# Top-8 replacement, exponentials and masks of the first expert layer by token quarter, with masks on GpSimd in both layers

## What is computed

```python
logits = jnp.einsum('bsd,ed->bse', x, gate_w) + gate_b
probs = jax.nn.softmax(logits, axis=1)                 # over the 4096 tokens
vals, idx = jax.lax.top_k(probs.transpose(0, 2, 1), K)  # K = 8
...
pooled = jnp.einsum('bked,bke->bed', gathered, topv)   # weighted sum of the 8 tokens
h = jax.nn.gelu(...pooled, weight1...)
out = ...h, weight2...
weighted = jnp.einsum('beo,bke->bkeo', out, topv)      # scattered back to the 8 tokens
```

## Time and profile before

| | before |
|---|---|
| device time, median of 3 runs | 574.76 us (574.59 to 575.63) |
| the profiled execution's own time | 575.6 us |
| its span in the profile | 573.8 us |
| TensorE busy | 533.4 us (93%) |
| VectorE busy | 333.3 us (58%) |
| ScalarE busy | 296.9 us (52%) |
| GpSimd busy | 63.6 us (11%) |

### The profile page before, as it was taken

One profiled execution on the slowest core, in us unless ns is written; L12 is line 12 of the kernel. 1 busy time (PEld: TensorE's weight loads), 2 busy tenths in 40 slices (PEclk: granted clock), 3 DMA queues, 4 the chain that ended last, 5 costly groups with the idle time before them and its releaser, 6 DMA issues.

```text
span 573.8 us, 26756 instructions
## 1 busy us (share of the span) xinstructions
PE 533.4 (93%) x11432; PEld 494.5 (86%) x11432; DVE 333.3 (58%) x826; ACT 296.9 (52%) x762; POOL 63.6 (11%) x62
## 2 busy tenths in 40 slices
PE   8889899899997999899999999989999999977895
PEld 8889899899996895689999999989999999976782
DVE  2767686635459926874445444434544455389826
ACT  4556575732278502465555555576666555567300
POOL 4000000020021000000000033320000044640000
PEclk9999999999999888999999999999999999999978
DMA  9941782330000000000000024330000244410007
GB/s 353 376 149 55 270 336 83 137 159 2 1 2 0 2 22 0 2 1 3 2 0 0 4 61 103 76 39 3 0 0 2 47 76 70 78 29 1 2 3 292
DMA packets 48159, 40.80 MB, mean 71 GB/s; under 512 B 42554, under 2 KB 42810, under 8 KB 46877
## 3 DMA queue, kind: packets, MB, share of 16 engines
q1 hardware_dynamic: 46606, 37.27, 20.2%
q0 software_dynamic: 1344, 2.17, 1.8%
q10 hardware_dynamic: 144, 0.39, 0.2%
HBM read 27.49 MB, written 4.19 MB: 55 GB/s over the span
## 4 chain that ended last, share of the span: by engine, by line
PE 70%; DVE 18%; ACT 3%; SPq 2%; POOL 2%; issue 2%; DMA 1%; DVEq 0%; ACTq 0%
PE PS L769 34%; PE PS L557 6%; PE PS L469 4%; PE PS L430 4%; PE PS L603 3%; PE PS L686 3%; PE PS L633 3%; PE PS L762 3%; DVE sums L1084 2%; PE PS L537 2%; DVE RCD L1096 2%; PE PS L463 2%; PE PS L496 2%; DVE sums L966 2%; SPq L332 2%
## 5 line engine op out<-in xcount | busy, mean ns | idle before, releaser
L769 PE MATMUL PS<-RE,conv_sb 128*64 128x64 f32 x6048 | 228.7, 227 | 2.5 <-DVE RE L1198 2.0
L769 PEld LDWEIGHTS PS<-RE,conv_sb 128*64 128x64 f32 x6048 | 211.0, 137 | 11.7 <-DVE RE L1198 4.4
L1198 DVE SCALAR_TENSOR_TENSOR RE<-PS,RE 128x64 f32<-128x64 f32 x504 | 113.1, 225 | 120.9 <-PE PS L769 110.3
L762 PE MATMUL PS<-ones_bf,biasT 128*64 128x64 bf16 x1008 | 100.5, 192 | 0.5 <-DVE RE L1191 0.4
L902 ACT ACTIVATE RE<-RCD 128x128 f32 (+1 forms) x126 | 38.9, 310 | 52.1 <-DVE RE L1198 52.0
L762 PEld LDWEIGHTS PS<-ones_bf,biasT 128*64 128x64 bf16 x1008 | 60.0, 112 | 1.5 <-ACT RCD L798 0.5
L469 PE MATMUL PS<-warm 128*128 128x128 bf16 x524 | 39.1, 241 | 4.0 <-DVE ones_bf L961 1.5
L469 PEld LDWEIGHTS PS<-warm 128*128 128x128 bf16 x524 | 35.3, 109 | 5.4 <-ACT RB L882 1.6
L321 POOL DMA_DIRECT2D RE<-RCD x32 | 18.6, 588 | 181.7 <-ACT RCD L905 181.7
L902 ACT ACTIVATE RE<-RE 128x128 f32 (+1 forms) x63 | 26.6, 422 | 19.5 <-DVE RE L1198 17.2
L905 ACT COPY RB<-RE 128x128 f32 (+1 forms) x126 | 35.6, 283 | 1.5 <-DVE RE L1198 1.5
(11 more groups left out here) (120 smaller groups left out, 753.0 us busy)
## 6 DMA issues: line engine op xcount, KB each, us to landing
RE<-wspec SPq DMA_DIRECT2D x8, 2048.0 KB, 9.0
RA<-x_in SPq DMA_DIRECT2D x8, 512.0 KB, 7.4
RCD<-x_in SPq DMA_DIRECT2D x1, 4096.0 KB, 13.2
out<-RA SPq DMA_DIRECT2D x8, 512.0 KB, 3.5
RCD<-RB SPq DMA_DIRECT2D x48, 64.0 KB, 2.1
RCD<-RB SPq DMA_DIRECT2D x26, 32.0 KB, 1.9
conv_sb<-conv_w SPq DMA_DIRECT2D x1, 768.0 KB, 20.0
RE<-RCD SPq DMA_DIRECT2D x8, 96.0 KB, 4.1
```

The source lines that it names most:

```text
L762: pe.matmul(conv_bank(u, h)[MO * o:MO * (o + 1)], biasT[:, s, MO * o:MO * (o + 1)], ones_bf[:, :], start=True, stop=False)
L769: m = pe.matmul(conv_bank(u, h)[MO * o:MO * (o + 1)], conv_sb[:, s, d, MO * o:MO * (o + 1)], prev, start=False, stop=(d == 2))
L1198: dve.scalar_tensor_tensor(out=state[:, state_slot(s, u), k, 1:1 + HO], in0=conv_bank(u, h), scalar=0.0, in1=rowb[:, u, k], op0=ALU.max, o ...
```

## The change

In the first expert layer (`l == 0`):

- The one replacement over 4096 tokens becomes four over 1024. A replacement by value needs a list of 8 values to look for, and a quarter's list may hold only values that are chosen in it. Three instructions on 32 elements a partition make the four lists at once: the top 8 are replaced in a copy of `cand` (`unpicked`), the rest is turned into `MASKED` and the replaced ones into 0, and this is added to `cand` (`picks`). Each has to wait for the one before.
- The exponentials are taken by quarter, in the order 0, 2, 1, 3, each with its own sum in `expsum4`; a reduction adds the four, and `rsum` is made after the mask of quarter 1.
- Between the exponentials of quarters 0 and 2, ScalarE takes the exponential of `L2` of quarter 2 in place: zero where `MASKED` stands, and equal to `E` elsewhere. GpSimd then forms this quarter's weights as the difference `E - exp(L2)`.
- VectorE's order is: replacements 2 and 0, mask 0, replacement 1, mask 1, the sum and its inverse, scaling 0, replacement 3, mask 3, scalings 1, 2, 3.
- TensorE has 76 matmuls in its `keep_warm` in place of 110. It turns `rsum` after quarter 1 and its 14 warm matmuls, and spreads it after the turning of quarter 2.

In the second layer the replacement and the exponentials stay whole. ScalarE adds the exponentials of `L2` for quarters 2 and 3, GpSimd forms those two masks, and VectorE has only masks 0 and 1 ahead of its scalings. The order on TensorE is the one from before.

The diff, without the declarations of the new tiles and semaphores and three lines that call `masks(0)`, `masks(1)` and `wait_masked`:

```diff
@@ -256,6 +260,26 @@
         CW = (E, RC[:, TOK:2 * TOK])
+        POOL_MASKS = ((2,), (2, 3))
+        DVE_MASKS = ((0, 1, 3), (0, 1))
+        REPLACED = (2, 0, 1, 3)
+        EXPS = (0, 2, 1, 3)
+
+        def wait_masked(eng, l, g):
+
+            if g in POOL_MASKS[l]:
+                eng.wait_ge(s_mskp, len(POOL_MASKS[0]) * l + POOL_MASKS[l].index(g) + 1)
+            else:
+                eng.wait_ge(s_msk, len(DVE_MASKS[0]) * l + DVE_MASKS[l].index(g) + 1)
+
+        def wait_replaced(eng, l, g):
+
+            eng.wait_ge(s_rep, 5 if l else REPLACED.index(g) + 1)
+
+        def wait_exps(eng, l, g):
+
+            eng.wait_ge(s_exp, 5 if l else EXPS.index(g) + 1)
+
         def centred(l, g):
             return RB[:, 1024 * (7 - g):1024 * (8 - g)] if l else RA[:, 1024 * g:1024 * g + 1024]
@@ -338,6 +362,13 @@
             x2 = by_run(RC[:, TOK * bh:TOK * (bh + 1)], k).rearrange("p (o i) w -> p o i w", i=Q)
             eng.tensor_tensor(X3[:, k, bh], CO[:, k, :, :, bh].rearrange("p i w o -> p o i w"), x2,
                               ALU.add).then_inc(done, 1)
+
+        def mask(eng, l, g, done):
+
+            left, exps = part(L2, l, g), part(E, l, g)
+            chosen = CW[l][:, 1024 * g:1024 * g + 1024]
+            eng.scalar_tensor_tensor(out=run_rows(chosen) if l else chosen, in0=left, scalar=MASKED / 2,
+                                     in1=exps, op0=ALU.is_le, op1=ALU.mult).then_inc(done, 1)
         block = ctx.enter_context(nc.Block())
@@ -392,6 +423,14 @@
                     xc = centred(l, g)
                     pool.tensor_tensor(square[:, 1, 0:1024], xc, xc, ALU.mult).then_inc(s_sqp, 1)
+            def masks(l):
+                for n, g in enumerate(POOL_MASKS[l]):
+                    wait_exps(pool, l, g)
+                    pool.wait_ge(s_exl, len(POOL_MASKS[0]) * l + n + 1)
+                    chosen = CW[l][:, 1024 * g:1024 * g + 1024]
+                    pool.tensor_tensor(run_rows(chosen) if l else chosen, part(E, l, g), part(L2, l, g),
+                                       ALU.subtract).then_inc(s_mskp, 1)
+
             def split_bias():
                 pool.wait_ge(s_mix, 4 * 6)
                 pool.memset(brow, 0.0).then_inc(s_bz, 1)
@@ -671,9 +712,13 @@
                     group(G_LT[l] + g, [LT[:, 8 * g + n].rearrange("p h n -> p (h n)") for n in range(8)], None)
                 pe.wait_ge(s_ld, 4 * l + 4)
-                keep_warm(0, 110)
-                pe.wait_ge(s_rs, l + 1)
-                pe.transpose(PS[0:1, 6, 0:P], rsum[:, :], ident).then_inc(s_rt, 1)
+                def turn_rsum():
+                    pe.wait_ge(s_rs, l + 1)
+                    pe.transpose(PS[0:1, 6, 0:P], rsum[:, :], ident).then_inc(s_rt, 1)
+
+                keep_warm(0, 110 if l else 76)
+                if l == 1:
+                    turn_rsum()
                 def pool_tokens(g):
                     pe.wait_ge(s_wtd, 4 * l + g + 1)
@@ -697,7 +742,9 @@
                     m.then_inc(s_wt, 1)
                     if g < 2:
                         keep_warm(7, 14)
-                    if g == 1:
+                    if l == 0 and g == 1:
+                        turn_rsum()
+                    if g == 2 - l:
                         pe.wait_ge(s_rr, l + 1)
                         pe.matmul(PS[0:C, 7, 0:P], ones[:, :], rs_row[:, :], start=True, stop=True).then_inc(s_rb, 1)
                     if g >= 1:
@@ -882,7 +929,21 @@
                     act.activation(o, i, ACT.Identity, bias=gateb_sb[:, l:l + 1]).then_inc(s_ld, 1)
                 act.wait_ge(s_nm, l + 1)
-                act.activation(E, L[l], ACT.Exp, bias=negmax[:, :], accum_out=expsum[:, :]).then_inc(s_exp, 1)
+                def exps_of_left(g):
+                    left = part(L2, l, g)
+                    wait_replaced(act, l, g)
+                    act.activation(left, left, ACT.Exp, bias=negmax[:, :]).then_inc(s_exl, 1)
+
+                if l == 0:
+                    for n, g in enumerate(EXPS):
+                        act.activation(part(E, 0, g), part(L[0], 0, g), ACT.Exp, bias=negmax[:, :],
+                                       accum_out=expsum4[:, g:g + 1]).then_inc(s_exp, 1)
+                        if n == 0:
+                            exps_of_left(2)
+                else:
+                    act.activation(E, L[l], ACT.Exp, bias=negmax[:, :], accum_out=expsum[:, :]).then_inc(s_exp, 1)
+                    for g in POOL_MASKS[1]:
+                        exps_of_left(g)
                 act.wait_ge(s_rt, l + 1)
                 act.copy(rs_row[:, :], PS[0:1, 6, 0:P]).then_inc(s_rr, 1)
                 act.wait_ge(s_rb, l + 1)
@@ -1116,16 +1177,33 @@
                 dve.max(top8[:, :], cand[:, :]).then_inc(s_mx, 1)
                 dve.wait_ge(s_mx, l + 1)
                 dve.tensor_scalar(negmax[:, :], top8[:, 0:1], -1.0, None, ALU.mult).then_inc(s_nm, 1)
-                dve.match_replace(L2, top8[:, :], L[l], MASKED).then_inc(s_rep, 1)
-                dve.wait_ge(s_exp, l + 1)
-                dve.reciprocal(rsum[:, :], expsum[:, :]).then_inc(s_rs, 1)
-                dve.wait_ge(s_rep, l + 1)
-                def mask(g):
-                    left, exps = part(L2, l, g), part(E, l, g)
-                    chosen = CW[l][:, 1024 * g:1024 * g + 1024]
-                    dve.scalar_tensor_tensor(out=run_rows(chosen) if l else chosen, in0=left, scalar=MASKED / 2,
-                                             in1=exps, op0=ALU.is_le, op1=ALU.mult).then_inc(s_msk, 1)
-
+                def total_exps():
+                    dve.wait_ge(s_exp, 4)
+                    dve.tensor_reduce(expsum[:, :], expsum4[:, :], AX_X, ALU.add).then_inc(s_sel, 1)
+                    dve.wait_ge(s_sel, 4)
+                    dve.reciprocal(rsum[:, :], expsum[:, :]).then_inc(s_rs, 1)
+
+                if l == 0:
+                    dve.match_replace(unpicked[:, :], top8[:, :], cand[:, :], MASKED).then_inc(s_sel, 1)
+                    dve.wait_ge(s_sel, 1)
+                    dve.tensor_scalar(unpicked[:, :], unpicked[:, :], MASKED / 2, MASKED, ALU.is_gt,
+                                      ALU.mult).then_inc(s_sel, 1)
+                    dve.wait_ge(s_sel, 2)
+                    dve.tensor_tensor(picks[:, :], unpicked[:, :], cand[:, :], ALU.add).then_inc(s_sel, 1)
+                    dve.wait_ge(s_sel, 3)
+                else:
+                    dve.match_replace(L2, top8[:, :], L[l], MASKED).then_inc(s_rep, 1)
+                    dve.wait_ge(s_exp, 5)
+                    dve.reciprocal(rsum[:, :], expsum[:, :]).then_inc(s_rs, 1)
+
+                def replace(g):
+                    dve.match_replace(part(L2, 0, g), picks[:, 8 * g:8 * g + 8], part(L[0], 0, g),
+                                      MASKED).then_inc(s_rep, 1)
+
+                def mask_now(g):
+                    wait_replaced(dve, l, g)
+                    wait_exps(dve, l, g)
+                    mask(dve, l, g, s_msk)
                 def weigh(g):
                     dve.wait_ge(s_wt, 4 * l + g + 1)
@@ -1135,19 +1213,24 @@
                                       .unsqueeze(4).to_broadcast([P, 8, BH, BL, NE]),
                                       ALU.mult).then_inc(s_wtd, 1)
-                mask(0)
-                mask(1)
-                if l == 1:
-                    mask(2)
-                    mask(3)
-                weigh(0)
                 if l == 0:
-                    mask(2)
-                weigh(1)
-                if l == 0:
-                    mask(3)
-                weigh(2)
-                weigh(3)
+                    replace(2)
+                    replace(0)
+                    mask_now(0)
+                    replace(1)
+                    mask_now(1)
+                    total_exps()
+                    weigh(0)
+                    replace(3)
+                    mask_now(3)
+                    weigh(1)
+                    weigh(2)
+                    weigh(3)
+                else:
+                    mask_now(0)
+                    mask_now(1)
+                    for g in range(4):
+                        weigh(g)
                 dve.wait_ge(s_pl, l + 1)
                 dve.wait_ge(s_rp, l + 1)
```

More of the change, by code:

```diff
@@ L71, in build_kernel @@
         cand, top8 = sb("cand", [P, 4 * 8]), sb("top8", [P, 8])
+        unpicked, picks = sb("unpicked", [P, 4 * 8]), sb("picks", [P, 4 * 8])
+        expsum4 = sb("expsum4", [P, 4])
         negmax, expsum, rsum = sb("negmax", [P, 1]), sb("expsum", [P, 1]), sb("rsum", [P, 1])
@@ L103, in build_kernel @@
         s_exp, s_rs, s_msk = sem("exps_ready"), sem("rsum_ready"), sem("weights_masked")
+        s_exl, s_mskp = sem("exps_of_left"), sem("weights_masked_pool")
+        s_sel = sem("picks_selected")
         s_wt, s_wtd = sem("weights_turned"), sem("weights_scaled")
@@ L411, in _ @@
             pool.memset(state, 0.0).then_inc(s_pad, 1)
+            masks(0)
             for n in range(len(MOVED)):
@@ L419, in _ @@
             squares(1)
```

(3 more changed lines are left out.)

## The result

| | before | changed |
|---|---|---|
| device time, median (4 executions each) | 575.19 us (574.59 to 575.80) | 572.38 us (571.11 to 582.96) |
| ratio to before | | 0.9944, 95% interval 0.9921 to 0.9966 |
| span of the profiled execution | 573.8 us | 570.5 us |

The kernel became 0.56% faster, more than the 0.2% that such a measurement can tell from no change; 0.22% was forecast, so the move is more than twice as large, and 572.38 us lie at the lower end of the stated range.

What follows compares the result with a forecast made beforehand. Each expert layer was bound by its own engine: TensorE in layer 0, VectorE's masks and first scaling in layer 1. Gains of 1.13 + 0.13 = 1.26 us gave 574.76 - 1.26 = 573.5 us, range 572.3 to 575.3.

Steps and rivals of the forecast that it cites:

- is mostly the recurrent convolution, which the change leaves alone: Whole kernel: TensorE makes up 70% of the chain, mostly in the convolution, so only the two expert layers count.
- The sum: Both expert layers: 1.13 + 0.13 = 1.26 us gained, 573.5 us forecast against the median.
- the rival on the clock: Layer 0 warm block: clock returns later, changed kernel's slack hides it, adding up to 1.3 us; 572.2 to 573.1, chance 0.19.
- Gain 1.13: Layer 1: VectorE loses masks 2 and 3 ahead of its first scaling; first product starts at 538.81 in place of 539.94.
- The rival in which GpSimd wins the operands: Layer 1: GpSimd starts ahead of VectorE's mask 1; whole change nil (574.8) or 1.0 us slower (575.8), chance 0.15.
- A two-input GpSimd instruction of 1024 took 1.89: GpSimd masks: 1.89 us where operands are contiguous, as in layer 0; 2.89 with permuted strides.
- The estimate of 2.25 us: GpSimd mask of 1024 by the skill's figure: ends 0.36 later, layer 0 loses 0.23, whole gain 0.90.
- Gain 0.13: Layer 0: products end at 207.96 in place of 208.09; replacement 3 and mask 3 ahead of scaling 1 cost the earlier start.
- Layer 0 costs more than counted: Layer 0: slower VectorE steps or a GpSimd mask of 2.25 to 2.89 take 0.4 to 1.0 off; 573.9 to 574.5, chance 0.23.
- if the idle time ahead of quarter 1 brings the clock down: Layer 0, TensorE idle about 1.3 us ahead of quarter 1: named as a way to be wrong, without a size.
- The lock: VectorE and GpSimd masks can't run together; layer 0's mask 1 waits until 195.28, has 1.10 left, ends 0.47 later than free.
- the assumption that replacements don't contend: VectorE beside GpSimd's masks: replacements and reductions, having one input, aren't held up; replacements taken at 1.21 us each.

Runs made afterwards that it cites:

- both fillings: Two runs of the changed kernel with TensorE's wait for mask 1 of layer 0 filled by warm matmuls: 571.21 us (0.9968) and 570.41 us (0.9955).
- the first filling: Changed kernel with 30 warm matmuls more (44 in place of 14) behind the turning of quarter 0 in layer 0; 571.21 us, ratio 0.9968.
- the second: Changed kernel, layer 0: 8 wide warm matmuls in TensorE's wait for mask 1, 65 narrow and 3 wide ahead in place of 76 narrow; 570.41 us, 0.9955.

## Why the prediction was off

- **The whole.** 1.26 us forecast, 2.8 measured between medians. The step that failed is the first: TensorE's chain "is mostly the recurrent convolution, which the change leaves alone". The sum has no term for anything outside the two layers, and gives no reason beyond this. The runs showed in its place that the convolution became 2.46 us shorter in the profile of the result (2.3 to 3.0 in the profiles of all kernels that have both counts) by the number of instructions ahead of it on VectorE and TensorE: two kernels that change one number each show half of it each, and one that changes both, with nothing of the change in it, shows 2.26 us. Of the 3.3 us of span, layer 1 gave 1.13, the convolution 2.46, and layer 0 nothing once the convolution starts; a clock that can stay down comes on top.
- **Inside the range by luck.** 572.38 us lie in the band of the rival on the clock (572.2 to 573.1). That rival had a clock that comes back later in the warm block; the convolution, not this, brought the time there.
- **Layer 1, "Gain 1.13".** Right: 19.49 to 18.36. The exponential took 1.15 us and VectorE kept the operands, 532.81 (its mask 1) against 532.96 (GpSimd). The rival in which GpSimd wins the operands occurred in none of the profiles.
- **The price of GpSimd, "A two-input GpSimd instruction of 1024 took 1.89".** The size of this term was wrong. That instruction squares: it reads one tile as both inputs. The mask reads two tiles and took 2.31 (193.40, when VectorE let go, to 195.71). It also subtracts where the other multiplies, and which of the two makes it longer wasn't tried. The groups by form of the kernel before, GpSimd, have a better row, an instruction of two tiles with 512 elements (busy us in all and mean ns of one, then idle time ahead):

```profile
L401 POOL TENSOR_TENSOR RE<-RE,biasT 128x512 f32<-128x512 f32 x1 | 1.2, 1155 | 0.1
```

  Twice 1155 ns is 2.31 us. The estimate of 2.25 us from the 4497 ns of the Trainium skill's "GPSIMD Engine Reference", section 3.1, which I set aside for the 1.89, was the nearer one. In layer 1 the two strided masks took 4.51 us behind VectorE's (534.03 to 538.54), 2.26 each, so the strides of 16-element runs cost nothing here.
- **Layer 0, "Gain 0.13".** It is a loss of 0.39 with the clock up (19.42 against 19.03, both fillings), mostly those 0.42 us: mask 1 ended 7.77 us behind `negmax` where the working had 7.29. This is the rival "Layer 0 costs more than counted", hidden in the total. VectorE's chain of small instructions, replacements and masks was right within 0.1 up to the start of mask 1.
- **"if the idle time ahead of quarter 1 brings the clock down"** stood in the prediction as a way to be wrong, with no price. It does: 1.2 us of loss in layer 0 in the profile of the result (20.58 against 19.42), and about 10 us when the clock stays down. That 1.5 us were made up behind layer 0 in that profile isn't owed to the fall or to the change: that stretch took 48.9 or 49.0 us in the kernel with 34 warm matmuls fewer and in the first filling too, and 50.3 in the second, all with the clock up in layer 0. My rival on the clock looked for the gain of a late rise in the warm block; the working had TensorE idle for 1.33 us ahead of quarter 1 (measured 1.79) and put no price on it.
- **The lock** on operands works as the earlier trace rows had it: mask 1 started at 194.63 and ended 1.08 us behind GpSimd (forecast 1.10). The replacement beside GpSimd's mask (193.39) took 1.21 us like the others, so the assumption that replacements don't contend held.

What stays open is why the counts matter. That it is the place of the loops' code fits (the first half's delay comes once a turn of VectorE's loop), but no run shows code being fetched, and why TensorE's count decides how long ScalarE waits for a DMA isn't shown at all. How the delay depends on the count between the values tried wasn't tried either.

## What to carry to other kernels

Before putting a gain down to an edit, cut both profiles at landmarks outside it: here a loop of hundreds of microseconds ran 1% faster because some instructions stood or didn't stand in front of it, and a kernel with dummy instructions alone shows such a gain for what it is. Try the smallest part of an edit alone: 34 warm matmuls fewer gave layer 0 more than the whole first version did. When work is taken off an engine's path, look for the wait that it opens on TensorE and price the clock there; fill the gap with warm matmuls, and count them. To price a two-tile instruction on GpSimd, take a row that reads two tiles, and don't run it beside a two-operand instruction that VectorE's chain depends on: here one mask more on VectorE beat one on GpSimd.

## What the runs showed of the hardware that I had not expected

- 10 tiny VectorE instructions ahead of a hardware loop made one 57 us sweep of it 1.3 us shorter. The two sweeps of the first half took 115.0 to 115.6 us in every profile with about 10 instructions more there, and 116.7 to 116.9 in every other.
- 34 TensorE instructions fewer took a DMA wait of 2.0 us in the hand-over 180 us later down to 0.3.
- The granted clock, once down ahead of the narrow products, stayed at 1.2 GHz for over 30 us with TensorE's records wholly busy.
- A GpSimd `tensor_tensor` over 1024 float32 elements took 1.89 us as the square of one tile and 2.31 as the difference of two.
